# VectorE's leaky part written into PSUM ahead of the mask products of a graph attention kernel

## What is computed

```python
h = jnp.maximum(_layernorm(x), 0.0)
# layer 0, attention; item_embs = h, V = entity_embs
scores = (h @ W @ a1)[:, None] + (V @ W @ a2)[None, :]
e = jnp.where(scores > 0, scores, 0.2 * scores)
e = jnp.where(adj > 0, e, -9e15)
x = x + elu(softmax(e, axis=1) @ V + h)
# layer 1
h = jnp.maximum(_layernorm(x), 0.0)
x = x + relu((adj.T @ h) @ U.T / adj.sum(axis=0)[:, None])
```

## Time and profile before

| | us |
|---|---|
| median of 3 runs | 402.12 (400.76 to 402.92) |
| span of the profiled execution | 399.7 |
| PE busy | 350.8 (88%) |
| DVE busy | 305.2 (76%) |
| ACT busy | 258.7 (65%) |
| POOL busy | 154.5 (39%) |

### The profile page before, as it was taken

How to read it: one execution, slowest core, us unless ns; L and a number is a source line. 1 busy time by engine, 2 the same in 40 slices (tenths; PEclk the granted TensorE clock), 3 DMA queues, 4 the chain that set the end, 5 groups by cost and what they waited for, 6 DMA issues and landing times.

```text
span 399.7 us, 15175 instructions
## 1 busy us (share of the span) xinstructions
PE 350.8 (88%) x7003; PEld 220.2 (55%) x7003; DVE 305.2 (76%) x419; ACT 258.7 (65%) x322; POOL 154.5 (39%) x136
## 2 busy tenths in 40 slices
PE   1716999799999888889999989989997899999996
PEld 0712565454445464535455534445544448999996
DVE  8799899759998598889967989998889761307433
ACT  2402699799997888799889999967775760110000
POOL 8775385584220771130051130032569682210000
PEclk9958699999999999999999999999999999999999
DMA  9999999999999999971000010002001004201110
GB/s 168 130 108 109 108 107 114 130 107 108 109 139 104 105 107 104 103 83 50 2 4 3 4 55 3 3 8 53 3 3 29 2 4 80 55 2 32 41 23 18
DMA packets 26806, 25.18 MB, mean 63 GB/s; under 512 B 22041, under 2 KB 22105, under 8 KB 26742
## 3 DMA queue, kind: packets, MB, share of 16 engines
q0 software_dynamic: 4752, 16.90, 40.7%
q1 hardware_dynamic: 19830, 6.75, 7.7%
q10 hardware_dynamic: 2160, 0.56, 0.8%
HBM read 72.76 MB, written 2.11 MB: 187 GB/s over the span
## 4 chain that ended last, share of the span: by engine, by line
PE 44%; DVE 25%; POOL 10%; issue 9%; ACT 6%; DMA 5%; SPq 0%; POOLq 0%; DVEq 0%
DVE scratch L882 15%; PE w L1249 13%; PE q L1364 10%; PE q L1224 9%; PE den L1257 4%; PE w L1364 4%; DMA adj_sb<-in_adj_dram 3%; POOL adj_sb L425 3%; DVE arena L934 3%; ACT q L724 2%; ACT arena L710 2%; DMA bi<-rows_sb 1%; PE den L1364 1%; POOL adj_sb L429 1%; POOL stat_c L470 1%
## 5 line engine op out<-in xcount | busy, mean ns | idle before, releaser
L882 DVE CUSTOM_DVE_ANT_0 scratch<-adj_sb,t_row 125x2048 uint8<-125x2048 uint8 x66 | 152.9, 2317 | 4.6 <-DMA adj_sb<-in_adj_dram 1.7
L1249 PE MATMUL w<-arena,v_sb 128*32 128x500 f32 (+3 forms) x1120 | 128.8, 508 | 2.3 <-issue 1.3
L1224 PE MATMUL q<-bi,adj_sb 128*32 128x125 bf16 (+1 forms) x3360 | 93.1, 220 | 15.2 <-ACT q L724 7.7
L1224 PEld LDWEIGHTS q<-bi,adj_sb 128*32 128x32 fp8e4 (+1 forms) x3360 | 70.8, 97 | 63.6 <-ACT q L724 32.2
L706 ACT ACTIVATE arena<-q,t_col 128x1000 f32<-128x1000 f32 (+2 forms) x102 | 88.4, 871 | 7.9 <-PE q L1224 7.6
L1257 PE MATMUL den<-arena,ones 128*32 128x250 f32 (+1 forms) x960 | 80.5, 342 | 0.0
L1257 PEld LDWEIGHTS den<-arena,ones 128*32 128x32 f32 x960 | 38.2, 111 | 49.8 <-issue 45.2
L710 ACT ACTIVATE arena<-arena,t 128x1000 f32<-128x1000 f32 (+2 forms) x38 | 40.8, 1073 | 18.6 <-DVE arena L934 18.4
L724 ACT ACTIVATE q<-second_row,minus_b 128x750 f32<-128x750 f32 (+1 forms) x49 | 48.1, 981 | 1.3
L724 ACT ACTIVATE q<-arena,minus_b 128x375 f32<-128x375 f32 (+1 forms) x53 | 42.3, 800 | 1.3
L1364 PE MATMUL q<-g_all,adj_sb 124*128 124x129 f16 (+1 forms) x660 | 39.2, 220 | 0.0
(11 more groups left out here) (186 smaller groups left out, 376.8 us busy)
## 6 DMA issues: line engine op xcount, KB each, us to landing
adj_sb<-in_adj_dram POOLq DMA_DIRECT2D x33, 500.0 KB, 37.0
arena<-s_dram SPq DMA_DIRECT2D x2, 500.0 KB, 7.8
out_dram<-v_sb SPq DMA_DIRECT2D x10, 96.0 KB, 1.9
x_sb<-in_x_dram SPq DMA_DIRECT2D x1, 928.0 KB
v_sb<-x_dram SPq DMA_DIRECT2D x1, 768.0 KB, 5.3
v_sb<-n_L_gnn_entity_embs_dram ACTq DMA_DIRECT2D x2, 256.0 KB, 5.7
v_sb<-n_L_gnn_entity_embs_dram SPq DMA_DIRECT2D x2, 256.0 KB, 4.8
second_row<-s_dram SPq DMA_DIRECT2D x1, 500.0 KB, 4.3
```

The source lines that it names most:

```text
L882: nc.vector.tensor_tensor_reduce(out=junk[0:R, :], in0=adj_bytes[0:R, b, half], in1=t_row[0:R, half], scale=1.0 / ONE, scalar=0.0, op0=ALU ...
L1224: last = nc.tensor.matmul(q[n % Q_SLOTS][e:e + width, bank, start:start + R], weights, bi[:, i % BI_SLOTS, k, :], start=not ON_ACT[n] and ...
L1249: last = nc.tensor.matmul(att(i)[h * D + d:h * D + d + 32, 0:(k1 - k0) * R], v_sb[:, c, d:d + 32], e[:, k0 * R:k1 * R], start=first, stop= ...
```

## The change

For DVE's tiles, the sum is replaced by a write ahead of the products. DVE writes max(a, b) into the q slot with a tensor_scalar; PE adds the mask products on top as for ACT's tiles, now waiting for DVE (`summed`) first; the exponential reads PSUM. The slot is free once the exponential is done: relu and DVE's write of tile n wait for `exped` of tile n - 2. In DVE's queue, the write for tile n + 2 stands at the end of tile n's work, behind the guards and other work of tile n and ahead of that of tiles n + 1 and n + 2; before, the sum of tile n stood ahead of tile n's work. The repeated products of stages 0 and 1 go.

```diff
@@ -701,13 +701,9 @@
 
             def exponentials(n, nb, c):
 
-                if ON_ACT[n]:
-                    act.wait_ge(masked, n + 1)
-                    nc.scalar.activation(e_part(n, nb), part(q[n % Q_SLOTS], nb), ACT.Exp, bias=t_col[:, c:c + 1])\
-                        .then_inc(exped, 1)
-                    return
-                act.wait_ge(summed, sums_to(n + 1))
-                nc.scalar.activation(e_part(n, nb), e_part(n, nb), ACT.Exp, bias=t02[:, c:c + 1])\
+                act.wait_ge(masked, n + 1)
+                offset = t_col if ON_ACT[n] else t02
+                nc.scalar.activation(e_part(n, nb), part(q[n % Q_SLOTS], nb), ACT.Exp, bias=offset[:, c:c + 1])\
                     .then_inc(exped, 1)
 
             def relu(n):
@@ -715,7 +711,7 @@
                 i, c = TILES[n]
                 nb = GROUPS[i][1] - GROUPS[i][0]
 
-                if n >= Q_SLOTS and ON_ACT[n - Q_SLOTS]:
+                if n >= Q_SLOTS:
                     act.wait_ge(exped, n - Q_SLOTS + 1)
                 if n < Q_SLOTS:
                     act.wait_ge(r1_ready, 1)
@@ -925,14 +921,17 @@
                 dve.wait_ge(r1_hi_done, i + 1)
                 nc.vector.tensor_tensor(low, whole, high, ALU.subtract).then_inc(r1_ready, 1)
 
-            def scores(n, nb, i, c):
-
+            def scores(n):
+
+                i, c = TILES[n]
+                nb = GROUPS[i][1] - GROUPS[i][0]
                 if c == min(DVE_TILES[i]):
                     wait_for_row(dve, i)
                     dve.wait_ge(t_scaled, 3)
-                dve.wait_ge(masked, n + 1)
-                nc.vector.scalar_tensor_tensor(out=e_part(n, nb), in0=a_part(i, nb), scalar=b_col[:, c:c + 1],
-                                               in1=part(q[n % Q_SLOTS], nb), op0=ALU.max, op1=ALU.add).then_inc(summed, 1)
+                if n >= Q_SLOTS:
+                    dve.wait_ge(exped, n - Q_SLOTS + 1)
+                nc.vector.tensor_scalar(part(q[n % Q_SLOTS], nb), a_part(i, nb), b_col[:, c:c + 1], None, ALU.max)\
+                    .then_inc(summed, 1)
 
             def copy_den(i):
 
@@ -1014,8 +1013,6 @@
                         sum_s(0)
             row_shifts(0)
             for n, (i, c) in enumerate(TILES):
-                if not ON_ACT[n]:
-                    scores(n, GROUPS[i][1] - GROUPS[i][0], i, c)
                 for b, h in guards_at(i, c):
                     guard(b, h)
                 if i >= 1:
@@ -1067,6 +1064,8 @@
                         copy_s(i + 1)
                     if at('range', i, c):
                         row_shifts(i + 1)
+                if n + Q_SLOTS < len(TILES) and not ON_ACT[n + Q_SLOTS]:
+                    scores(n + Q_SLOTS)
             copy_den(NI - 1)
             normalise(NI - 1)
             elu(NI - 1)
@@ -1206,29 +1205,16 @@
                     pe.wait_ge(bi_loaded, 32 * i)
                 if ON_ACT[n]:
                     pe.wait_ge(relued, relus_to(n + 1))
-                elif n >= Q_SLOTS and ON_ACT[n - Q_SLOTS]:
-                    pe.wait_ge(exped, n - Q_SLOTS + 1)
-                elif n >= Q_SLOTS:
-                    pe.wait_ge(summed, sums_to(n - Q_SLOTS + 1))
+                else:
+                    pe.wait_ge(summed, sums_to(n + 1))
                 nb = b1 - b0
-                in_bank = nb // 2 if nb > 4 else nb
                 width = MASK_COLUMNS[i]
-
-
-                again = not ON_ACT[n] and nb < 8
                 for k in range(nb):
                     bank, start = place(nb, k)
-                    closes = start == (in_bank - 1) * R
                     for e in range(0, P, width):
                         weights = adj_sb[:, b0 + k, c * P + e:c * P + e + width]
                         last = nc.tensor.matmul(q[n % Q_SLOTS][e:e + width, bank, start:start + R], weights, bi[:, i % BI_SLOTS, k, :],
-                                                start=not ON_ACT[n] and start == 0, stop=ON_ACT[n] or (closes and not again),
-                                                skip_group_check=ON_ACT[n])
-                    if again and closes:
-                        for e in range(0, P, width):
-                            weights = adj_sb[:, b0 + k, c * P + e:c * P + e + width]
-                            last = nc.tensor.matmul(q[n % Q_SLOTS][e:e + width, bank, in_bank * R:4 * R], weights,
-                                                    bi[:, i % BI_SLOTS, k, :], start=False, stop=True)
+                                                start=False, stop=True, skip_group_check=True)
                 last.then_inc(masked, 1)
 
             def attend(n, i, c):
```

## The result

The changed kernel takes 413.86 us, median of 4 runs (412.96 to 414.73), against 402.52 for the kernel before on the same chip: ratio 1.0277, 95% interval 1.0244 to 1.0311, 11.3 us slower. The forecast was 410.5 with a range of 401.5 to 415.5. The profiled spans are 412.5 and 399.7.

The account below looks back on a forecast made before the run. Handoffs between three in-order queues bound stages 2 to 4, no engine being full. Terms 0.8 + 0.4 - 1.8 + 1.9 + 1.2 + 1.4 + 0.6 + 3.9 = +8.4 took the profiled 399.7 to 408.1, plus 2.4 to 410.5 us; range 401.5 to 415.5.

Parts of the forecast that it names:

- rival (b): All stages: the write runs at two columns a cycle, 0.73 us; near 397.4 us in all; chance 0.05.
- Stage 0 to 1: Write 0.29 moves ahead of variance(2), delaying POOL's pow, scale and write 0.31, so mask 1.0 starts later: +0.8 us.
- tiles 3.8 to 3.12: Write 3.10, now ahead of guard 9, makes DVE wait 1.9 us for the exponential of tile 3.8: +1.4 us.
- Stage 2 to 3: Writes 2.23, 2.27 and 2.29 move ahead of guards and row_shifts(3), which ends later: +1.9 us.
- stage 2: Tiles 2.6, 2.8, 2.12 and 2.14 lose ACT's waits, 3.1 us, of which some comes back: -1.8 us.
- Rival (a): Waits go and queue places cost nothing, as DVE always finds exponentials done: 397.1 us; chance 0.08.
- (c): Rival: slack takes up the losses of stages 0 to 3 and only stage 4 pays: 406.0 us; chance 0.20.
- (d): Rival: PE hides the longer slot in stage 4 and the stage ends are taken up: 402 us; chance 0.09.
- Stage 1 to 2: Two writes of 0.99 us stand ahead of row_shifts(2); POOL's later loads of adj cost nothing, at most 2.3: +0.4 us.
- Stage 3 to 4: Write, mask and exponential of 3.28 follow row_shifts(4), where the sum had its mask done: +0.6 us.
- Stage 4: Slot held until its exponential is done, 3.11 us a pair: floor +2.9, lost spare time +1.0, together +3.9 us.
- The tail: PE's gather products at the end start after the last exponential and only shift: 0 us.

Follow-up runs that it names:

- e7: The kernel before with the new way for tiles 2.6, 2.8, 2.12, 2.14 and 2.23 alone, writes two tiles ahead: 403.29 us, ratio 1.0014.
- e4: The kernel of e2 with the writes at the place in DVE's queue where the sum stood: 407.38 us, ratio 1.0127 to the kernel before.
- e2: The new way in stages 0 to 3 alone (27 tiles), stage 4 keeping the sum: 411.82 us, ratio 1.0244 to the kernel before.
- e5: The changed kernel with variance(2) ahead of the write of 0.29 in DVE's queue: 411.31 us, ratio 1.0222 to the kernel before.
- e6: The kernel of e5 with scale(3) moved behind the write of 1.31: 411.48 us, ratio 1.0228 to the kernel before.
- e1: The new way in stage 4 alone (31 tiles), stages 0 to 3 keeping the sum: 406.88 us, ratio 1.0121 to the kernel before.
- e3: The changed kernel with the product that turns the shifts ahead of mask 3.28 in PE's queue: 412.54 us, ratio 1.0262 to the kernel before.
- e12: The kernel before with the new way for tiles 3.4 to 3.12 alone, writes where the sum stood: 401.32 us, ratio 0.9960.

## Why the prediction was right or wrong

Right: the direction, the range, and most of the mechanism. The write takes 1.259 us for 1000 columns (1.25 taken; the low end 0.73 of rival (b) is out) and 0.997 for 750, so 1.05 ns a column. The Trainium skill (VectorE: DVE Perf Modes, "Why PSUM operands drop a tier") holds fp32 with a PSUM operand at one element a cycle, and the trace agrees: the write, with PSUM as its output alone, gains nothing on the sum's 1.253. The loop in stage 4 is 3.14 (3.11). Stage 0 to 1 is +0.7 (0.8), first tiles of stage 3 +1.3 (1.2), tiles 3.8 to 3.12 +1.4 (1.4) with the wait of DVE at the named place, 2.17 (1.9). Stage 2 to 3, +2.6 (1.9), is in reach: row_shifts(3) at 204.4 is 4.8 late.

Right by luck: stage 2, -1.8 (-1.8). The forecast had the gain at tiles 2.6 to 2.14, whose waits of ACT would go. There the changed kernel gains 0.1: mask 2.0 is 3.9 late and exponential 2.14 3.8. The rest comes behind 2.14, where the lateness falls from 3.8 to 2.1. row_shifts(2) was only 2.4 late, so DVE, whose guards fill that stretch, was less late than the mask of 2.0, and the stage caught up with it: from row_shifts(2) to exponential 2.27 it is 71.1 us before and 70.9 after. e7, whose stage 2 begins in time, gains at 2.9 and has lost it by 2.27.

Rival (a), places that cost nothing, fell with e4: the same writes at another place are 4.4 us cheaper. Rivals (c) and (d) fell with e2.

The forecast was 8.4, the runs show 11.3 and the profiles 12.8. The forecast put 3.9 of it into stage 4 and had the first mask of that stage some 4 us late; it is 11.4 late (271.32 and 282.77). Four terms were mis-sized:

- Stage 1 to 2, +0.4 in the sum, +3.2 measured. The step that failed is "POOL's loads ... I cost that at nothing". The loads were covered as said; what stands behind them in the same queue, close_sum(0), was not looked at, and VectorE waits for it. e5 takes it away and gives 2.2 us back. The upper bound written for it, 2.3, was near. A second part is that the write of 1.31 stands behind scale(3): e6 moves the mask of 2.0 by 1.1. Of the 3.2, the 1.5 by which mask 2.0 is later than row_shifts(2) is what stage 2 took up again.
- Stage 3 to 4, +0.6 against +2.5. The sum had the write, mask and exponential of 3.28 in a row, but not that turn_halves stands behind them in PE's queue, nor that PE's stand of 2.3 us is followed by half clock. By the estimate above the clock is 1.5 of the 1.9 missed; e4, where PE stands 1.80 and the clock stays up, adds 0.5.
- Stage 4, +3.9 against +1.6. The floor rose a little more than said, by 3.3 and not 2.9 (16 pairs at 3.14); the stalls didn't stay. From exponential 3.31 to 4.31 it is 56.1 us before and 57.7 after. That is 9.2 over the floor before and 7.5 after, where the forecast kept its 10.1, taken over a window of 57.0, and added 1.0. DVE's other work in the stage took 43.99 - 37.27 = 6.7 us instead of 9.4: three steps that are held by one of POOL's (below) took 2.29, 2.30 and 1.84 before and 0.75, 1.44 and 1.55 after. The 1.0 for lost spare time shows nowhere as a term of its own.
- The tail, 0 against +1.1. "The tail (PE's gather products) starts after the last exponential and only shifts" is the step that failed. It starts after POOL's last addition, which also waits for the attend of 4.30, and an exponential that no longer has a sum ahead of it doesn't make PE's queue any earlier. From exponential to addition it is 1.45 us against 0.29 before; e1, with the new way in stage 4, has 1.45, and e2, without it there, 0.27.

The four errors are +2.8, +1.9, -2.3 and +1.1, and the rest, 0.9, is rounding and stage 2 to 3. So the closeness of 410.5 owes something to errors of opposite sign, and the +2.8 and the agreement in stage 2 are one matter: over both stages the forecast had -1.4 and the profile shows +1.4.

## What to carry to other kernels

When a step is pulled forward in an in-order queue, follow every queue that it delays to the last instruction that somebody waits for, past transfers that are covered: here some 2 of the 11 us stood twenty instructions down on POOL. Buying an early handoff pays only where the engine that gives it reaches the step with its input done; the same write cost 11 us over all tiles two tiles early, and gained 1.4 on five tiles at the old place, where DVE waited for nobody. Judge an edit at a border by the end of the next stretch, not by the first event behind it. And when a term comes out as forecast, look whether it did so at the instructions that it named.

## What the runs showed of the hardware

A stand of PE of some 2 us can cost more than itself. Behind the 2.32 us of the changed kernel, and behind 1.16 and 0.95 close together in e3, the granted clock was at 0.50 for 3.4 us; behind 1.80 in e4 it stayed at 1.00. The same holds in stage 2: behind stands of 1.96 near 170 us in e2, e3, e4 and e6 the clock was at 0.50 for 3.4 us, behind 1.69 in the changed kernel it was not. The length of the stand doesn't settle it. Ahead of the mask of 0.31, e3 and the changed kernel run the same instructions and PE stands 1.72 in both; the first window is e3, the second the changed kernel:

```profile
79.60:83.00 3.40, 3.40 (x36) 2.05 (x34) 1.55 (x3) 2.56 (x4) 3.26 (x3) 0.50 1.00 107
```

```profile
79.60:83.00 3.40, 3.34 (x57) 2.30 (x57) 1.86 (x4) 2.89 (x4) 3.18 (x4) 1.00 1.00 107
```

Small VectorE steps were held while a POOL step ran that had begun before them. POOL's step first, then VectorE's, in the kernel before:

```profile
264.18 1.12 POOL L534 TENSOR_TENSOR g_all<-buf_a,g_all 125x512 f16<-125x512 f32 x1 [26.88 <-ACT buf_a L700]
...
264.28 1.04 DVE L916 TENSOR_TENSOR neg_t<-neg_t,low_t 125x8 f32<-125x8 f32 x1
```

```profile
286.81 2.33 POOL L550 TENSOR_TENSOR t_row<-t_row 128x1000 f32<-128x1000 f32 x1
```

```profile
287.39 2.29 DVE L974 SCALAR_TENSOR_TENSOR x_sb<-buf_a,x_sb 125x512 f32<-125x512 f32 x1
```

The 8-column step ends with POOL's, at 265.3, and takes 0.17 where none runs (263.29 in e12). The 512-column one ends 0.54 us after POOL's, at 289.68. In the changed kernel the same step starts only 0.21 us before such a POOL step (297.50 to 299.83) ends. It too ends 0.54 after it, and so takes 0.75:

```profile
299.62 0.75 DVE L973 SCALAR_TENSOR_TENSOR x_sb<-buf_a,x_sb 125x512 f32<-125x512 f32 x1
```

A step that starts ahead of POOL's isn't held: that at 206.10 in the earlier trace rows begins 0.20 before a POOL step and takes its 0.69. The sums, which have one side in PSUM, take 1.24 to 1.26 us in the 34 cases beside a POOL step of over 0.9 us and 1.25 to 1.26 in the 17 without. The Trainium skill (GPSIMD Engine Reference, "Specifications") names such contention for VectorE instructions with two SBUF inputs or in a two-port mode; the held steps shown here have two SBUF inputs, so the rows agree. It was read from timelines, not tested by a run of its own.
